# One fused kernel of six layers: first rows and job order of the scan, Silu, sums and store by halves, statistics behind the scan

## The chip, the cores and the metric

One Trainium2 chip, one NeuronCore. The metric is the device time of one execution in microseconds (us), as the median of several runs. Engines: PE multiplies matrices, DVE (VectorE) and POOL (GpSimd) do elementwise work, ACT (ScalarE) applies functions and copies, SP issues the DMAs. All run at once and wait for each other by semaphores.

## The reference

On x of 8 x 256 tokens with 256 features each, six layers in a row, each on a layernorm of x and added to it: a half-weighted mixture of experts, a Mamba layer with a selective scan, the same mixture again, a half-weighted SwiGLU feed-forward, causal attention with ALiBi, and the feed-forward again.

```python
x = x + 0.5 * moe(layernorm(x))
x = x + mamba(layernorm(x))
x = x + 0.5 * moe(layernorm(x))
x = x + 0.5 * ffn(layernorm(x))
x = x + attention(layernorm(x))
x = x + 0.5 * ffn(layernorm(x))

# moe, ffn: (silu(x @ Wg) * (x @ Wu)) @ Wd; the moe weights each expert's part by its gate
# the scan within mamba, for 512 channels and 16 states, over 256 steps of each sequence:
s = exp(delta * A) * s + delta * B * u
y = sum over states of s * C, then (y + D * u) * silu(gate) @ Wout
```

## The kernel before, in words

**Tiling.** The 2048 tokens are four chunks of 512; a chunk has two pairs of 128-token tiles. x stays in SBUF as tile X. The normed and transposed x is kept in two parts, high and low (xnT_hi, xnT_lo); a product is made of three matmuls, high by high, high by low, low by high (`three`, lines 161 to 163).

**Between two layers (class Tail).** A pair of tiles goes through `stats` on DVE (bn_stats, bn_aggr), `pool` (rstd by a power, on POOL), `norm` (DVE; in the scan's tail for chunks 0 and 1 it is ACT, lines 288 to 294, and POOL then has four operations in place of two), `pe` (transpose), `act` (the high part, a copy out of PSUM), `low` (DVE, the low part). The entry into the first layer is class Entry: `chunk` issues the loads of x by chunks on SP's queue, between the loads of the first weight tiles; `vector`, `scalar` and `tensor` are written out by hand in order, so their line order is each engine's order.

**Mixture and feed-forward (class Glu).** The hidden features come in tiles of 128: 25 tiles in 6 groups (2, 4, 4, 5, 5, 5) in a mixture, 8 in a feed-forward. A step j is one tile for one chunk: 100 steps in each mixture, 32 in each feed-forward. In a step, `gu` makes 12 matmuls of 512 columns: six into the gate half, then six into the up half; `down` makes 12 of 256 columns for the step before, into the sum banks 5 (first pair of tiles) and 6 (second pair). ACT takes Silu of the gate half (`scalar`, line 778). DVE multiplies with the up half; in tiles with gates (all but the first two of a mixture) it multiplies the up half with the gate rows first (line 827). ACT copies the high part (784), DVE makes the low part (850), and `down` of that step waits for it. `take` (DVE) adds the sum banks to X at the end of a chunk. After the last step of the kernel `Tail.sync` stores X chunk by chunk.

**The scan (class Scan).** 128 units q, 32 for each chunk c: 16 states for channels 0 to 255 (h = 0), then 16 for channels 256 to 511 (h = 1). r is q modulo 32. In a unit, ACT writes the decays into two PSUM banks (`decays`, two activations, line 1551), POOL writes the inputs into one of four state buffers (`inputs`, line 1208), DVE runs the recurrence (`scan`, line 1618) and multiplies with C (`weigh`, line 1625), for which PE has spread a row of C to all partitions (`spread`, line 1421), and PE sums the result over states (y, line 1437). PE's step q is: wait for weigh(q), spread(q + 1), y(q), then one *job* of the next or the last chunk, out of the tables `JOBS` (each pass), `START` (first chunk in its place) and `LAST` (last chunk). At n = 0 (r = 0 and 16) y also waits for the gate product (`gate`) that reads the sum of the half before.

**Jobs.** h, g: projections to the conv input and to the gate; v: the convolution, in two steps; xp, ms: projection and mean square for the norms; dt: step sizes; out: the output product of the chunk before (16 matmuls); ln: the tail's transpose. All use PSUM bank 7, one after the other: `vacant` waits until the job before has been read out of it (for g, by the Silu of `take` on ACT). v and g load the Silu table and load the other one again after it. A `DIAG` entry adds D * u to y after the job. ACT's order in a pass: decays(q + 2), take of the job of q - 1, then at fixed r `log` (three activations for the softplus), tail work. POOL's: `inputs(q + 3)`, with `lose`, `lost`, `step`, `times_u`, `normed`, `rows_lo` between, at fixed r. inputs(q) waits for y(q - 4), which frees its buffer.

**Where the scan hands over.** In the last chunk the tail's statistics of chunks 0 and 1 are made within the loop (r = 5, 12, 21, 23), as are POOL's rstd (r = 7, 14, 22, 24) and ACT's norm (r = 9, 16, 24, 26). After the loop PE makes the second mixture's first `gu`, then both output jobs, and DVE adds them. Chunks 1 to 3 are transposed in the mixture's first steps (class Reentry).

## Time and profile before

| | us |
|---|---|
| median of 3 runs | 1901.24 (1899.95 to 1901.25) |
| the profiled execution | 1902.52 |
| its span, by which the trace counts | 1900.7 |
| PE, DVE, ACT, POOL busy | 1808.4, 1333.8, 945.2, 581.2 |
| first mixture from, scan from, second mixture from | 12.8, 469, 970 |

Busy time is what an engine's instructions take; where it is full, nothing else can be sooner. A bracket behind a row of the timeline says how long the engine stood idle before it and what ended that. The mean granted clock of PE is 0.993 of full speed.

### The profile page before, as it was taken

To read this page: it belongs to the slowest core of one execution; us is meant where nothing else is said; L and a number is where in the kernel's file an instruction comes from. 1 tells how busy PE (TensorE), PEld (TensorE's weight loads), DVE (VectorE), ACT (ScalarE), POOL (GpSimd) and SP (SyncE) were. 2 spreads that over 40 slices of the span, in tenths; PEclk is the share of its full clock that TensorE was granted. 3 is DMA by queue.
4 is the path that set the end of the run, shared out by engine and by line. 5 is a ranking of instruction groups with operands and counts; after the bars stand their busy time and mean duration, and the time that the engine had idled before them with its cause. 6 is when DMAs were issued, how large, how long until landed. Compare 5 with 4: busy or idle time off the path is not lost.

```text
span 1900.7 us, 26241 instructions
## 1 busy us (share of the span) xinstructions
PE 1808.4 (95%) x9417; PEld 1375.2 (72%) x9417; DVE 1333.8 (70%) x1870; ACT 945.2 (50%) x1782; POOL 581.2 (31%) x399
## 2 busy tenths in 40 slices
PE   7999999999799999988689999999999999999998
PEld 6888888888354544534267888888888887777887
DVE  6666656567999999999976666565675556666533
ACT  3442323333688677684445433233333338888422
POOL 1000234000489878888720000000000025555000
PEclk9999999999899999999999999999999999999999
DMA  5332344220222222223202233232121306553100
GB/s 197 90 98 66 97 145 136 64 62 23 67 73 70 69 72 77 71 71 108 72 17 76 72 95 105 65 104 63 64 77 44 65 1 147 109 109 68 37 12 23
DMA packets 84186, 146.39 MB, mean 77 GB/s; under 512 B 13848, under 2 KB 23704, under 8 KB 83544
## 3 DMA queue, kind: packets, MB, share of 16 engines
q1 hardware_dynamic: 84056, 144.72, 26.6%
q8 instruction: 75, 1.23, 0.3%
q14 instruction: 55, 0.45, 0.1%
HBM read 130.38 MB, written 14.29 MB: 76 GB/s over the span
## 4 chain that ended last, share of the span: by engine, by line
PE 72%; DVE 14%; issue 6%; ACT 4%; POOL 3%; DMA 0%; DVEq 0%; SPq 0%; POOLq 0%; ACTq 0%
PE psum L161 19%; PE psum L162 18%; PE psum L163 18%; DVE scan_state L1618 6%; PE psum L1437 5%; POOL scan_state L1208 2%; PE psum L1990 1%; PE psum L1361 1%; DVE scan_state L1625 1%; PE psum L1332 1%; ACT attn_p L2138 1%; DVE X L807 1%; DVE moe_hidden_lo L850 1%; PE psum L1421 1%; PE psum L278 1%
## 5 line engine op out<-in xcount | busy, mean ns | idle before, releaser
L1208 POOL TENSOR_TENSOR scan_state<-scan_delta_u,scan_B_rows 128x1024 f32<-128x1024 f32 x127 | 299.5, 2368 | 95.3 <-PE psum L1437 81.2
L161 PE MATMUL psum<-xnT_hi,moe_w_hi 128*128 128x512 f32 x800 | 316.5, 396 | 2.7 <-DVE xnT_lo L470 2.6
L778 ACT ACTIVATE moe_hidden<-psum 128x512 f32<-128x512 f32 x200 | 119.5, 597 | 393.9 <-PE psum L163 393.9
L162 PE MATMUL psum<-xnT_lo,moe_w_hi 128*128 128x512 f32 x800 | 314.2, 393 | 0.0
L163 PE MATMUL psum<-xnT_hi,moe_w_lo 128*128 128x512 f32 x800 | 312.0, 390 | 0.0
L1618 DVE TENSOR_TENSOR_SCAN scan_state<-psum,scan_state 128x1024 f32<-128x1024 f32 x128 | 292.2, 2283 | 4.2 <-POOL scan_state L1208 3.0
L827 DVE TENSOR_TENSOR moe_gated_up<-moe_gate_rows,psum 128x512 f32<-128x512 f32 x184 | 126.5, 688 | 210.0 <-PE psum L163 124.8
L1437 PE MATMUL psum<-scan_state,ident 128*128 128x512 f32 x512 | 248.1, 608 | 3.8 <-DVE scan_gated L1633 2.6
L418 POOL TENSOR_SCALAR rstd<-mean_var 128x2 f32<-128x2 f32 x48 | 10.5, 220 | 752.8 <-DVE mean_var L452 752.5
L161 PE MATMUL psum<-moe_w_hi,moe_hidden_hi 128*128 128x256 f32 x800 | 230.4, 288 | 3.9 <-DVE moe_hidden_lo L850 2.6
L163 PE MATMUL psum<-moe_w_hi,moe_hidden_lo 128*128 128x256 f32 x800 | 226.3, 283 | 0.0
L162 PE MATMUL psum<-moe_w_lo,moe_hidden_hi 128*128 128x256 f32 x800 | 226.3, 283 | 0.0
L1551 ACT ACTIVATE psum<-scan_delta,scan_A 128x510 f32<-128x510 f32 x256 | 165.4, 679 | 117.5 <-DVE scan_state L1618 114.6
L784 ACT ACTIVATE moe_hidden_hi<-moe_hidden 128x512 fp32r<-128x512 f32 x200 | 126.3, 631 | 168.0 <-DVE moe_hidden L831 165.7
L850 DVE TENSOR_TENSOR moe_hidden_lo<-moe_hidden,moe_hidden_hi 128x512 fp32r<-128x512 f32 x200 | 138.2, 691 | 73.7 <-ACT moe_hidden_hi L784 72.1
L163 PEld LDWEIGHTS psum<-xnT_hi,moe_w_lo 128*128 128x128 f32 x800 | 150.7, 188 | 33.1
L161 PEld LDWEIGHTS psum<-xnT_hi,moe_w_hi 128*128 128x128 f32 x800 | 151.4, 189 | 30.1 <-issue 4.0
L162 PEld LDWEIGHTS psum<-xnT_lo,moe_w_hi 128*128 128x128 f32 x800 | 151.5, 189 | 24.1 <-issue 0.2
L161 PEld LDWEIGHTS psum<-moe_w_hi,moe_hidden_hi 128*128 128x128 f32 x800 | 152.5, 191 | 17.6 <-issue 6.3
L1625 DVE TENSOR_TENSOR scan_state<-scan_state,psum 128x1024 f32<-128x1024 f32 x128 | 156.2, 1220 | 7.0 <-PE psum L1421 3.0
L1437 PEld LDWEIGHTS psum<-scan_state,ident 128*128 128x128 f32 x512 | 98.3, 193 | 84.0 <-issue 69.5
L162 PEld LDWEIGHTS psum<-moe_w_lo,moe_hidden_hi 128*128 128x128 f32 x800 | 152.6, 191 | 7.8 <-issue 1.4
(226 smaller groups left out, 3476.4 us busy)
## 6 DMA issues: line engine op xcount, KB each, us to landing
scan_B_rows<-scan_B SPq DMA_DIRECT2D x127, 256.0 KB, 3.1
moe_gate_rows<-gate_table SPq DMA_DIRECT2D x176, 128.0 KB, 3.0
moe_w_raw<-moe_pack SPq DMA_DIRECT2D x50, 384.0 KB, 4.0
attn_stack<-attn_rows SPq DMA_DIRECT2D x96, 128.0 KB, 5.3
moe_gate_rows<-gate_table SPq DMA_DIRECT2D x32, 224.0 KB, 3.1
ffn_w_raw<-ffn_pack SPq DMA_DIRECT2D x16, 384.0 KB, 3.6
moe_gate_rows<-gate_table SPq DMA_DIRECT2D x32, 160.0 KB, 2.6
moe_gate_rows<-gate_table SPq DMA_DIRECT2D x24, 192.0 KB, 2.8
```

The lines of the kernel that those rows point to most:

```text
L161: e.matmul(out, wH, xH, start=start, stop=False)
L162: e.matmul(out, wH, xL, start=False, stop=False)
L163: return e.matmul(out, wL, xH, start=False, stop=stop)
L778: e.activation(self.hb[:, b, :], self.k.psum[:, 2 * b, :], ACT.Silu).then_inc(self.s_silu.sem, 1)
L784: e.activation(self.hH[:, b, :], self.hb[:, b, :], ACT.Copy).then_inc(self.s_hH.sem, 1)
L827: e.tensor_tensor(self.tu[:, b, :], self.gp[:, at, :], k.psum[:, 2 * b + 1, :], ALU.mult).then_inc(self.s_tu.sem, 1)
L850: e.tensor_tensor(self.hL[:, b, :], self.hb[:, b, :], self.hH[:, b, :].bitcast(F32), ALU.subtract).then_inc(self.s_hL.sem, 1)
L1208: e.tensor_tensor(self.st[q % self.NBUF][:], self.dtu[:, 2 * h:2 * h + 2, :], self.Bs[:, q % self.RING, :].unsqueeze(1).broadcast_to([P, 2 ...
L1437: x = e.matmul(ps[:, 4 + m, :], k.ident[:], self.st[q % self.NBUF][:, m, :], start=(n == 0), stop=(n == NST - 1))
L1551: x = e.activation(ps[:, 2 * (q % 2) + m, :].rearrange("p (s t) -> p s t", s=2)[:, :, 1:], self.delta[:, i, :].rearrange("p (s t) -> p s t ...
L1618: e.tensor_tensor_scan(st, ps[:, b:b + 2, :].rearrange("p b t -> p (b t)"), st, 0.0, ALU.mult, ALU.add).then_inc(self.s_scan.sem, 1)
L1625: e.tensor_tensor(st[:], st[:], ps[:, 6, :].unsqueeze(1).broadcast_to([P, 2, CHUNK]), ALU.mult).then_inc(self.s_z.sem, 1)
```

## The change

1. **Load.** x's first chunk comes as two loads of 256 rows with a semaphore each.
2. **Entry's order.** ACT splits the first weight tile before its first copy; DVE makes the low weight and both low parts before the statistics of chunk 1.
3. **Silu by half.** `gu` signals after the gate half (s_gs), and Silu waits for that; DVE waits for the whole (s_gu) in tiles without gates.
4. **Last sums and store by halves.** For the last chunk of the last layer the first pair of tiles is added once bank 5 is done, and each pair is stored by itself.
5. **Statistics behind the scan.** Those of chunk 1 come after the last gate, with POOL's rstd and ACT's norm in the next layer.
6. **Job order of the scan.** out1 from r = 10 to 6 (its sum from 12 to 8), v1 to 8 and 9, h2 and h3 to 10 and 11; g0, g1 of the first chunk from 10, 11 to 6, 7; g2, g3 from 25, 26 to 19, 25; h0, h1 from 29, 30 to 26, 29; the D products of channels 2, 3 from 19 to 20 and 21.
7. **n = 0.** At r = 0 and 16 the job comes before the wait for the gate and before y.

```diff
 # Tail
-        for c in range(NCH):
+        for c in range(NCH - 1):
             e.wait_ge(self.s_add.sem, self.s_add.at(2, c))
             e.dma_start(self.out[c * CHUNK:(c + 1) * CHUNK, :].rearrange("(n p) f -> p n f", p=P),
                         self.k.X[:, 4 * c:4 * c + 4, :]).then_inc(self.s_store.sem, 16)
-        e.wait_ge(self.s_store.sem, 16 * NCH)
+        for p in range(2):
+            e.wait_ge(self.s_add.sem, self.s_add.at(p + 1, NCH - 1))
+            rows = slice((TILES - 4 + 2 * p) * P, (TILES - 2 + 2 * p) * P)
+            e.dma_start(self.out[rows, :].rearrange("(n p) f -> p n f", p=P),
+                        self.k.X[:, TILES - 4 + 2 * p:TILES - 2 + 2 * p, :]).then_inc(self.s_store.sem, 16)
+        e.wait_ge(self.s_store.sem, 16 * (NCH + 1))
...
 # Glu
-        m.then_inc(self.s_gu.sem, 1)
+            m.then_inc((self.s_gu if half else self.s_gs).sem, 1)
...
+            if n == 1 and self.tail.last and j == self.N - 1:
+                m.then_inc(self.s_half.sem, 1)
...
-            e.wait_ge(self.s_gu.sem, self.s_gu.at(j + 1))
+            e.wait_ge(self.s_gs.sem, self.s_gs.at(j + 1))
...
+            if by_half and p == 0:
+                e.wait_ge(self.s_half.sem, self.s_half.at(1))
+            elif by_half:
+                e.wait_ge(self.s_dn.sem, self.s_dn.at(self.N))
...
             else:
+                e.wait_ge(self.s_gu.sem, self.s_gu.at(j + 1))
                 e.wait_ge(self.s_silu.sem, self.s_silu.at(j + 1))
...
 # Entry
+        if c == 0:
+            for p, sem in enumerate((self.tail.s_in[0], self.tail.s_in2)):
+                e.dma_start(self.k.X[:, 2 * p:2 * p + 2, :],
+                            self.x[p * 2 * P:(p + 1) * 2 * P, :].rearrange("(n p) f -> p n f", p=P)
+                            ).then_inc(sem.sem, 16)
+            return
...
+        self.moe.split_hi(e, 0)
         for p in range(2):
             self.tail.act(e, 0, 2 * p + 1)
-            self.moe.split_hi(e, p)
+        self.moe.split_hi(e, 1)
...
+        self.moe.split_lo(e, 0)
+        t.low(e, 0, 0)
+        t.low(e, 0, 1)
         t.add(e, 1, 0)
         t.stats(e, 1, 0)
-        t.low(e, 0, 0)
-        self.moe.split_lo(e, 0)
-        t.low(e, 0, 1)
...
 # Scan
-    JOBS = {0: ("dt2", 0), 1: ("dt3", 0), 2: ("out0", -1), 4: ("v0", 1, 0), 5: ("v0", 1, 1), 6: ("v1", 1, 0),
-            7: ("v1", 1, 1), 8: ("h2", 1), 9: ("h3", 1), 10: ("out1", -1), 12: ("v2", 1, 0), 13: ("v2", 1, 1),
+    JOBS = {0: ("dt2", 0), 1: ("dt3", 0), 2: ("out0", -1), 4: ("v0", 1, 0), 5: ("v0", 1, 1), 6: ("out1", -1),
+            8: ("v1", 1, 0), 9: ("v1", 1, 1), 10: ("h2", 1), 11: ("h3", 1), 12: ("v2", 1, 0), 13: ("v2", 1, 1),
             14: ("v3", 1, 0), 15: ("v3", 1, 1), 16: ("xp0", 1, 0), 17: ("xp0", 1, 1), 18: ("ms0", 1),
-            20: ("dt0", 1), 21: ("dt1", 1), 22: ("xp1", 1, 0), 23: ("xp1", 1, 1), 24: ("ms1", 1),
-            25: ("g2", 0), 26: ("g3", 0), 27: ("g0", 1), 29: ("h0", 2), 30: ("h1", 2), 31: ("g1", 1)}
-    START = {2: ("h0", 1), 3: ("h1", 1), 10: ("g0", 0), 11: ("g1", 0)}
-    DIAG = {0: (0,), 1: (1,), 19: (2, 3)}
+            19: ("g2", 0), 20: ("dt0", 1), 21: ("dt1", 1), 22: ("xp1", 1, 0), 23: ("xp1", 1, 1), 24: ("ms1", 1),
+            25: ("g3", 0), 26: ("h0", 2), 27: ("g0", 1), 29: ("h1", 2), 31: ("g1", 1)}
+    START = {2: ("h0", 1), 3: ("h1", 1), 6: ("g0", 0), 7: ("g1", 0)}
+    DIAG = {0: (0,), 1: (1,), 20: (2,), 21: (3,)}
...
             if n == 0 and q:
                 e.wait_ge(self.s_z.sem, self.s_z.at(q + 1))
                 spread(q + 1)
+                if self.job(q):
+                    job(self.job(q), self.BANK)
                 e.wait_ge(self.s_yg.sem, self.s_yg.at(2 * c + h))
...
-            if self.job(q):
+            if self.job(q) and (n or not q):
                 job(self.job(q), self.BANK)
...
-            if c and r in (4, 12):
+            if c and r in (4, 8):
                 add(c - 1, 0 if r == 4 else 1)
...
-            if c == NCH - 1 and r in (5, 12, 21, 23):
-                self.tail.stats(e, r // 20, int(r in (12, 23)))
+            if c == NCH - 1 and r in (5, 12):
+                self.tail.stats(e, 0, int(r == 12))
         gate(NCH - 1, 1)
+        for p in range(2):
+            self.tail.stats(e, 1, p)
         for p in range(2):
             add(NCH - 1, p, self.ENDS[p])
```

POOL's and ACT's tail work of chunk 1 leaves the scan's loop in the same way; `Glu.pool` of the second mixture starts at chunk 1, and `Reentry.act` makes ACT's norm of chunk 1 at its step 0, ahead of the copies.

## Rows read from the trace of the kernel before

**Rows 1.** The page: PE's busy tenths in 40 slices; one stretch of the busy times.

```profile
PE   7999999999799999988689999999999999999998
...
469.00:970.00 501.00, 446.34 (x1175) 212.61 (x1173) 478.14 (x325) 347.58 (x475) 385.34 (x186) 0.97 0.23 71
```

**Rows 2.** Chain of waits (first row) and timeline, 0 to 13: start, length, engine, line.

```profile
1.43 3.81 DMA X<-x
...
8.65 2.04 PE L278 MATMUL psum<-ident,x_stage 128*128 128x128 f32 x8 [8.65 <-DVE x_stage L460]
...
10.27 0.83 ACT L751 ACTIVATE moe_w_hi<-moe_w_raw 128x768 fp32r<-128x768 f32 x1
...
11.00 0.59 ACT L298 ACTIVATE xnT_hi<-psum 128x512 fp32r<-128x512 f32 x1
...
12.84 0.77 PE L161 MATMUL psum<-xnT_hi,moe_w_hi 128*128 128x512 f32 x1 [2.15 <-DVE xnT_lo L470]
```

**Rows 3.** Timeline of DVE in the scan: two recurrences, one unit apart.

```profile
558.10 2.28 DVE L1618 TENSOR_TENSOR_SCAN scan_state<-psum,scan_state 128x1024 f32<-128x1024 f32 x1
...
561.55 2.28 DVE L1618 TENSOR_TENSOR_SCAN scan_state<-psum,scan_state 128x1024 f32<-128x1024 f32 x1
```

**Rows 4.** Timeline of DVE in the scan: its longer waits.

```profile
611.44 2.29 DVE L1618 TENSOR_TENSOR_SCAN scan_state<-psum,scan_state 128x1024 f32<-128x1024 f32 x1 [0.97 <-POOL scan_state L1208]
...
630.66 0.69 DVE L1638 TENSOR_TENSOR X<-X,psum 128x512 f32<-128x512 f32 x1 [1.68 <-PE psum L1361]
...
660.17 0.69 DVE L1638 TENSOR_TENSOR X<-X,psum 128x512 f32<-128x512 f32 x1 [1.31 <-PE psum L1361]
...
747.77 0.69 DVE L1638 TENSOR_TENSOR X<-X,psum 128x512 f32<-128x512 f32 x1 [0.31 <-PE psum L1361]
```

**Rows 5.** Chunk boundary: PE's busy time and granted clock; y; ACT's Silu of g1.

```profile
616.00:620.00 4.00, 3.83 (x5) 0.59 0.26 95
734.00:738.00 4.00, 3.36 (x8) 1.00 0.30 106
...
616.17 3.24 PE L1437 MATMUL psum<-scan_state,ident 128*128 128x512 f32 x4 [0.64 <-DVE scan_gated L1633]
...
616.37 0.60 ACT L1494 ACTIVATE scan_silu_gate<-psum 128x512 f32<-128x512 f32 x1
```

**Rows 6.** First chunk: y in the chain of waits; ACT's decays, and a g.

```profile
523.35 1.72 PE psum L1437 x4
...
525.32 1.30 ACT L1551 ACTIVATE psum<-scan_delta,scan_A 128x510 f32<-128x510 f32 x2
...
545.02 0.60 ACT L1494 ACTIVATE scan_silu_gate<-psum 128x512 f32<-128x512 f32 x1
545.63 1.28 ACT L1495 ACT_TABLE_LOAD   x1
```

**Rows 7.** Timeline of POOL: the inputs that start its chain of 11 operations.

```profile
585.30 2.36 POOL L1208 TENSOR_TENSOR scan_state<-scan_delta_u,scan_B_rows 128x1024 f32<-128x1024 f32 x1 [1.59 <-PE psum L1437]
```

**Rows 8.** Timeline of DVE: statistics within the loop; the last output's sum.

```profile
931.75 0.75 DVE L448 BATCH_NORM_STATS2 bn<-X 128x6 f32<-128x256 f32 x2
...
932.75 2.29 DVE L1618 TENSOR_TENSOR_SCAN scan_state<-psum,scan_state 128x1024 f32<-128x1024 f32 x1
...
976.67 0.69 DVE L1638 TENSOR_TENSOR X<-X,psum 128x512 f32<-128x512 f32 x1 [4.98 <-PE psum L1361]
```

**Rows 9.** The end: chain of waits (first row), timeline; stores by size and us to landing.

```profile
1890.26 0.23 PE psum L161
...
1894.41 0.39 PE L161 MATMUL psum<-ffn_w_hi,ffn_hidden_hi 128*128 128x256 f32 x1 [1.37 <-DVE ffn_hidden_lo L850]
...
1896.15 1.29 DVE L807 SCALAR_TENSOR_TENSOR X<-psum,X 128x512 f32<-128x512 f32 x2 [1.79 <-PE psum L163]
...
out<-X SPq DMA_DIRECT2D x4, 512.0 KB, 2.8
attn_rows<-attn_rows_hi SPq DMA_DIRECT2D x16, 256.0 KB, 2.0
```

More of the change, by code:

```diff
@@ L197, in __init__ @@
         if entry:
+            self.s_in2 = Sem(k, "in0b")
             self.s_in = [Sem(k, f"in{c}") for c in range(NCH)]
@@ L433, in add @@
             e.wait_ge(self.s_in[c].sem, self.s_in[c].at(16))
+            if c == 0 and p:
+                e.wait_ge(self.s_in2.sem, self.s_in2.at(16))
         if not self.back:
@@ L533, in __init__ @@
         self.s_gu = Sem(k, "gu", total=N)
+        self.s_gs = Sem(k, "gs", total=N)
         self.s_silu = Sem(k, "silu", total=N)
@@ L539, in __init__ @@
         self.s_dn = Sem(k, "dn", total=N)
+        self.s_half = Sem(k, "dn_half") if tail.last else None
         self.s_acc = Sem(k, "acc", total=NCH * (self.NG - 1))
@@ L656, in pool @@
     def pool(self, e):
-        for c in range(2 if self.guest else NCH - 1 if self.handed else NCH, NCH):
+        for c in range(1 if self.guest else NCH - 1 if self.handed else NCH, NCH):
             for slot in (0, 2):
@@ L801, in take @@
         c, last = n % NCH, n - NCH * (self.NG - 1)
-        e.wait_ge(self.s_dn.sem, self.s_dn.at(self.ends(n)))
+        by_half = self.tail.last and n == NCH * self.NG - 1
+        if not by_half:
+            e.wait_ge(self.s_dn.sem, self.s_dn.at(self.ends(n)))
         if n >= NCH:
@@ L1004, in pe, with act @@
         super().pe(e, j)
+    def act(self, e, j):
+        if j == 0:
+            for p in range(2):
+                self.tail.act(e, 1, 2 * p)
+        super().act(e, j)
 class Scan:
@@ L1233, in pool @@
                 self.next.split_lo(e, q + 5 - self.N)
-            if c == NCH - 1 and r in (7, 14, 22, 24):
-                self.tail.pool(e, r // 20, 2 * (r in (14, 24)))
+            if c == NCH - 1 and r in (7, 14):
+                self.tail.pool(e, 0, 2 * (r == 14))
         if not self.next:
@@ L1589, in scalar @@
                 log(c + 1, 0)
-            if c == NCH - 1 and r in (9, 16, 24, 26):
-                self.tail.act(e, r // 20, 2 * (r in (16, 26)))
+            if c == NCH - 1 and r in (9, 16):
+                self.tail.act(e, 0, 2 * (r == 16))
             if r == 27 and c + 1 < NCH:
@@ L1679, in vector @@
                 gate((q - 1) // self.UNITS, 0 if r else 1)
-            if c == NCH - 1 and r in (5, 12, 21, 23):
-                self.tail.stats(e, r // 20, int(r in (12, 23)))
+            if c == NCH - 1 and r in (5, 12):
+                self.tail.stats(e, 0, int(r == 12))
         gate(NCH - 1, 1)
+        for p in range(2):
+            self.tail.stats(e, 1, p)
         for p in range(2):
```

## The prediction

> **What bounds the kernel now.** I read the busy times first. In the mixtures of experts and the feed-forwards (slices 2 to 9, 21 to 32 and 38 to 39 of 40) PE's digit is 9, so an edit pays there only where PE stands: at the start, at a seam, at the end. In the scan DVE is full (478 of 501 us) and PE is not (446) [rows 1]. Then I read each stage's timeline. To PE's first projection, at 12.84, a chain runs from the load of x over statistics, transposes and ScalarE's copies [rows 2]. In the scan one unit of DVE (recurrence, weighting) starts every 3.45 us [rows 3], and only a few rows show DVE standing [rows 4]. In the last 9 us one tile's chain drains alone [rows 9]. The sum is made against the profiled execution (1902.5 us, span 1900.7), which lies 1.3 above the median of 1901.24; I apply it to the median. A measurement of this kernel tells about 0.2%, 3.8 us, from no change.
>
> **First rows.** The load of 512 KB takes 3.81 us [rows 2]. Halved, its first half can land sooner by up to its share of the moving time; I take 0.7 (bounds 0 and 1.3), the second no sooner, and SP issues one DMA more (0.4 us), behind which the first weight tile still lands before ACT wants it. Statistics and rstd of pair 0 move forward, pair 1 follows on POOL, so both transposes come 0.7 sooner. ACT now splits the weight ahead of its copies: before, the split (0.83 from 10.27) held the second copy back to 11.00, though its transposes ended at 10.69 [rows 2]. DVE had statistics and the low weight ahead of the second low part and now has only the weight, done while the copy runs. So that low part (0.7), which PE waits for, ends at 10.75 + 0.6 + 0.7 = 12.05, with the load's share at 11.4, and no longer at 12.8: PE starts 1.3 sooner. That stretch runs at the lower clock, and the clock need not rise sooner with it, and DVE owes two pairs of statistics (1.0 each, by [rows 8]), one norm and one split before the first product, which it then reaches some 1.2 sooner. **-1.2** (-0.6 to -1.6); PE carries it through the first mixture.
>
> **Silu by half.** 232 steps get an earlier Silu, but PE is full there [rows 1], and gated tiles wait for DVE's own product anyway: nothing, while PE's queue covers it. It counts where PE has run dry: at the second mixture's start, -0.3 (0 to -0.7), and at the end. There PE stood 1.37 for the chain Silu, product, high, low [rows 9]. Silu (0.6) leaves that chain: -0.65. The last sums: two instructions in 1.29 after PE's last matmul; half of it now runs beside PE's second half: -0.6. Store: 512 KB lands in 2.8, a store of 256 KB in 2.0 [rows 9]; half remains at the end: -0.5 (0 to -0.8). **-1.75**.
> The Trainium skill (DMA: Bandwidth & Descriptors, Anatomy of one DMA) puts most of a DMA's fixed cost in its completion, which halving does not shorten; by that rule only the moving time of half the bytes goes.
>
> **Statistics behind the scan.** Two pairs leave DVE's loop in the last chunk, 1.00 each from 931.75 to 932.75. They go between the last gate and the last sums, where DVE stands 4.98 [rows 8]. POOL's and ACT's share go with them, into 6 us in which both stand. **-2.0**, and covered: 2.0 fits in 5. Without that cover they would cost the same again.
>
> **Job order of the scan.** Four things, by step r of 32.
> (a) r = 0: the job moves ahead of y and of the wait for the gate. Before, PE stood there 0.6, and DVE later waited 1.68 for the output job [rows 4]. But the job dt2 takes the bank of g1, the job of r = 31, whose Silu runs at 616.37 to 616.97 [rows 5]. So PE cannot do the job in the gap: it stands until 617.0, then job and y. Against the old course (y from 616.17) that is worth 1.0 if PE is at its full clock, as y took 3.24 in place of 1.72 at a granted clock of 0.59. At the second boundary the clock stayed at 1.00 [rows 5], the later wait was 0.31 [rows 4], and there it costs 0.7. So: -1.35 over three boundaries with the clock up in all, +3.65 with it down in all (1.7 each). PE stands longer than before, which speaks for down; I take **+1.1**.
> The Trainium skill (TensorE: Matmul & The Clock Gate, Part 1) says that the clock follows recent activity and that its phase varies from run to run. By that rule each boundary is a throw; the rows agree in that two alike idles gave different clocks.
> (b) out1 from r = 10 to 6, its sum from 12 to 8. DVE waited 1.31 for it in two chunks [rows 4], PE being late after six full steps; now two are ahead. Bounds 0 and 1.31 each; I leave 0.9: **-0.9** in all.
> (c) Chunk 0: g0, g1 move to r = 6, 7, behind log (r = 5) and v0. A g costs ACT its Silu and two table loads, 3.2, and the decays 1.3, over the unit's 3.45 [rows 6]. ACT: decays at 525.32, + 1.3 + load 1.3 + Silu 0.6: g0 leaves its bank at 528.5; second load, decays, load, Silu: g1 at 533.0. PE: y ends at 525.07, + projection 1.4 (six matmuls of 0.23 [rows 9]) + spread 0.2 + y 1.7: it wants g0's bank at 528.4, and by the same steps g1's at 532.0. PE is full in this chunk, so this 1.1 goes to DVE: **+1.1** (0 to 2.2).
> The Trainium skill (ScalarE: Activation LUTs, What ACT_TABLE_LOAD costs) counts 2.66 us for each switch with its drain. The rows show the next ACTIVATE 1.3 after a load starts; by the page (c) would be some 5 us.
> (d) g2 moves to 19, the two D products to 20 and 21, and at r = 16 the job stands ahead of y but waits 0.9 for v3's Silu. PE then is 0.5 to 0.8 later at y of step 23. That y starts POOL's chain: it waited 1.59 for it at 585.30 [rows 7], is then busy through 11 operations, and DVE waits 0.97 for its last [rows 4]. What y loses, DVE loses: **+1.8** over three chunks (0 to 2.5). That g2 is out of ACT's crowd at 26 to 28 helps only a wait that this one covers.
>
> **Sum:** -1.2 - 0.3 - 1.75 - 2.0 + 1.1 - 0.9 + 1.1 + 1.8 = -2.15; 1901.24 becomes **1899.1**. The bounds of this course reach from about -6 to +2.
>
> **Rival A, the scan's new order pays.** The clock holds at all boundaries (-1.35), chunk 0 absorbs ACT's crowd, POOL's chain starts where it did, and (b) gives all but 1.1: then the scan gives -1.35 - 1.5, the statistics -2.0, and start, seam and end -3.25 to -4.3: some -8.5, about 1893; with half of it, 1895. For it: the PE's slack of a unit (a spread is due only 2.3 us after its release, as long as a recurrence takes [rows 3]). Against it: the Silu rows of [rows 5, 6]. 28%.
>
> **Rival B, slower: PE's new waits take the clock.** Place: r = 0 and r = 16, where a job held for an eviction now stands ahead of y. At r = 0 PE stands 1.6 on end, at r = 16 0.9. If both bring the low clock, a boundary costs as in (a), +3.65, and at r = 16 PE falls 1.7 further behind, to 3 us against the 2.3 that a spread has: DVE loses 0.8 each in four chunks, 3.2, and POOL's chain starts later, +1.5. With (c), (d) and (b): +3.65 + 1.1 + 1.8 - 0.9 + 3.2 + 1.5 = 10.35, less 5.25 elsewhere: +5.1, 1906.3. It decides where the low clock comes at more than the three boundaries. For it: two of three are low already. Against: at the second boundary PE stood 0.6 of 4 us and kept its full clock [rows 5]. 7%.
>
> **Rival C, the start and the end do not pay.** The clock rises at the same time as before whatever starts sooner, x's halves land together, and the last store completes with its latency: the start gives 0.3, the end 1.0. Then -0.5: 1900.7. 12%, all of it within 0.2%.
>
> **Numbers.** The forecast has 53%, with C and A's weak part within 3.8 us: faster by over 0.2% 30% (A and the forecast's lower tail), within 62%, slower 8%. The range leaves out the far ends of A and B: 1894.3 to 1903.8.
>
> **What would show it.** PE's first projection near 11.5 and the Silu of it before its second half ends; dt2's bank wait at each boundary ending on scan_silu_gate, and the clock there; waits for L1361 at the second sum below 1.3; PE waits on scan_silu_gate in 528 to 533; DVE's wait for POOL before step 32 above 0.97; no stall at the seam beyond 5 us for the moved statistics; the last store alone behind 1896. I am wrong if DVE's waits in the scan shrink in sum by over 4 us, or if PE waits nowhere for an eviction.

## The result, and the profile after

The changed kernel takes 1906.55 us (1905.25 to 1907.61) where the kernel before, on the same chip, took 1901.96 (1899.95 to 1905.45): a ratio of 1.0021, 95% interval 1.0011 to 1.0030. Measured again on another chip it was 1906.03 against 1903.32, 1.0018 (1.0009 to 1.0027). It is slower, by 2.7 to 4.6 us (0.2%), where 1899.1 and 2.15 us faster were forecast, and it lies outside the range of 1894.3 to 1903.8. The profiled execution took 1905.30, its span 1903.2, 2.5 more than the span of before.

**The start and the end** did what they should. First the timeline of the changed kernel's start (start, length, engine, line, operation, in brackets the idle time before it and what ended it):

```profile
4.33 0.75 DVE L456 BATCH_NORM_STATS2 bn<-X 128x6 f32<-128x256 f32 x2 [4.33 <-DMA X<-x]
...
7.61 2.04 PE L279 MATMUL psum<-ident,x_stage 128*128 128x128 f32 x8 [7.61 <-DVE x_stage L468]
...
8.73 0.60 ACT L299 ACTIVATE xnT_hi<-psum 128x512 fp32r<-128x512 f32 x1
...
9.69 0.60 ACT L299 ACTIVATE xnT_hi<-psum 128x512 fp32r<-128x512 f32 x1 [0.36 <-PE psum L279]
...
11.11 0.77 PE L161 MATMUL psum<-xnT_hi,moe_w_hi 128*128 128x512 f32 x1 [1.46 <-DVE xnT_lo L478]
```

PE transposes at 7.61 where [rows 2] had 8.65, the second copy starts at 9.69 where it was 11.00, and the first projection comes 1.73 sooner. Then the last waits, timeline of PE and DVE, and of the page's DMA issues the last store's (x count, size of one, us to landing):

```profile
1898.25 0.39 PE L161 MATMUL psum<-ffn_w_hi,ffn_hidden_hi 128*128 128x256 f32 x1 [0.74 <-DVE ffn_hidden_lo L869]
...
1899.27 1.41 DVE L825 SCALAR_TENSOR_TENSOR X<-psum,X 128x512 f32<-128x512 f32 x2 [1.07 <-PE psum L163]
```

```profile
out<-X SPq DMA_DIRECT2D x2, 256.0 KB, 2.1
```

PE stands 0.74 for its last hidden tile where [rows 9] had 1.37, the sums start while PE still works (DVE waited 1.07, not 1.79), and half a store lands in 2.1, not 2.8.

**The scan** took it all back. One stretch of it, PE's busy time (and number of instructions), then PEld, DVE, ACT, POOL, then granted clock, DMA share and GB/s:

```profile
468.00:974.00 506.00, 443.10 (x1170) 212.37 (x1168) 475.43 (x316) 344.28 (x469) 382.34 (x178) 0.98 0.22 70
```

The stretch is 5 us longer than that of [rows 1], and DVE is busy 475 us of it, no more than before: it waits more. DVE's longer waits now, in its timeline:

```profile
533.70 1.22 DVE L1659 TENSOR_TENSOR scan_state<-scan_state,psum 128x1024 f32<-128x1024 f32 x1 [1.42 <-PE psum L1453]
...
623.47 1.22 DVE L1659 TENSOR_TENSOR scan_state<-scan_state,psum 128x1024 f32<-128x1024 f32 x1 [0.99 <-PE psum L1453]
...
632.23 0.69 DVE L1672 TENSOR_TENSOR X<-X,psum 128x512 f32<-128x512 f32 x1 [1.68 <-PE psum L1393]
...
647.75 0.69 DVE L1672 TENSOR_TENSOR X<-X,psum 128x512 f32<-128x512 f32 x1 [1.14 <-PE psum L1393]
```

The first is in chunk 0, behind g0 and g1; the others follow the first chunk boundary: the weighting of step 2 (0.99, new), the sums of out0 (1.68, as in [rows 4]) and out1 (1.14; 1.31 before). The views that put numbers on all of it are the starts of the 128 recurrences: a step takes 3.45 us [rows 3], so what lies between two starts beyond that is what DVE lost or did besides. "The gap at step r" is the time from the start of recurrence r to that of r + 1, less 3.45. Summed by place, in us, from the timelines of three kernels (the third is the run undo_order, below):

```
                                        before   changed   undo_order
start of the first recurrence           495.44    493.41     494.36
chunk 0, steps 0 to 15                    2.15      3.89       1.42
steps 25 to 31, chunks 0 to 2             4.61      7.05       4.61
steps 2 to 4 of chunks 1, 2, 3       2.57 0.88 2.56  3.42 3.42 3.15  0.88 0.88 0.88
second output's sum, chunks 1 to 3        4.43      4.07       4.43
statistics in chunk 3                     4.0       2.0        2.0
first to last recurrence                469.42    475.25     463.28
last low part to the end of the span      7.01      5.70       5.72
```

The scan's gaps account for 5.8 of the 5.83 us that it is longer. The statistics' 2.0 are gone from it as planned, so the new order costs 7.8 (0.28 of it is the gap at step 2 of chunk 0, which differs from run to run, see the last section). The biggest row is that of the three boundaries, 9.99 where it was 6.01. One of them, PE and ACT from the changed kernel's timeline:

```profile
615.74 0.50 PE L1453 MATMUL psum<-scan_BC,scan_state_pick 128*128 128x512 f32 x1 [1.38 <-DVE scan_state L1659]
617.73 1.15 PE L1385 MATMUL psum<-scan_weighted,scan_Wdt 128*128 128x512 f32 x2 [1.49 <-ACT scan_silu_gate L1528]
618.70 3.58 PE L1471 MATMUL psum<-scan_state,ident 128*128 128x512 f32 x4
```

```profile
615.79 1.28 ACT L1528 ACT_TABLE_LOAD   x1
617.08 0.60 ACT L1528 ACTIVATE scan_silu_gate<-psum 128x512 f32<-128x512 f32 x1
```

and PE's busy time and granted clock in three stretches around it:

```profile
611.00:615.00 4.00, 3.37 (x11) 1.00 0.19 66
615.00:619.00 4.00, 1.76 (x4) 0.96 0.45 121
619.00:623.00 4.00, 4.00 (x7) 0.61 0.30 76
```

PE stands 1.38 for the weighting, then 1.49 for g1's Silu, which frees dt2's bank, and right behind that the clock falls to its lower level (1.2 GHz) and y takes 3.58. PE stands 1.49 for the Silu at the other two boundaries too. There the clock falls while dt2 runs: its two matmuls take 1.92 and 2.08, not 1.15, and y 2.82 and 2.40. The second profile of the changed kernel shows the same three. Before, y took 3.24 at the first [rows 5] and 3.61 at the third, and 1.99 at the second.

### The profile page after: what moved, and what is told of

Same layout as the page of the kernel before. It is cut to its first block, busy times and chain, and to the rows that moved or that the text cites. A ratio compares the mean times of both kernels' runs of the same rounds, so it can differ in the third digit from the quotient of the medians.

```text
span 1903.2 us, 26321 instructions
## 1 busy us (share of the span) xinstructions
PE 1807.4 (95%) x9417; PEld 1376.8 (72%) x9417; DVE 1333.9 (70%) x1870; ACT 945.9 (50%) x1782; POOL 579.5 (30%) x399
## 4 chain that ended last, share of the span: by engine, by line
PE 73%; DVE 13%; ACT 6%; issue 5%; POOL 2%; DMA 1%; SPq 0%; DVEq 0%; ACTq 0%; POOLq 0%
PE psum L161 19%; PE psum L162 19%; PE psum L163 18%; DVE scan_state L1652 5%; PE psum L1471 5%; PE psum L1393 1%; PE psum L2026 1%; PE psum L1373 1%; POOL scan_state L1240 1%; ACT attn_p L2174 1%; DVE moe_hidden_lo L869 1%; PE psum L1385 1%; DVE X L825 1%; DVE scan_state L1659 1%; PE psum L279 1%
```

## The experiments

Base is the changed kernel, where no other is named. The time of the kernel before behind each "against" was taken on the same chip; where a text says how far a run lies from the changed kernel, that is a difference of medians of different chips, on which the kernel before read 1901.96 to 1904.20. A "low boundary" is one at which the clock is at its lower level while y or the job ahead of it runs: y takes 2.4 to 3.6 us in place of 1.9 to 2.0, and the gap at step 4 is 2.25, in place of 0.88 (or 1.7, where the job is held).

**undo_order**: the whole of the scan's order back.

```diff
-    JOBS, START, DIAG as changed;  if c and r in (4, 8): add(...)
-                if self.job(q):                      # ahead of y at n == 0
-                    job(self.job(q), self.BANK)
+    JOBS, START, DIAG as before;   if c and r in (4, 12): add(...)
+            if self.job(q):                          # behind y
```

Expected:

> The changed kernel with the scan's order as before (job table, first chunk's table, D products, the second output sum at step 12, the job of steps 0 and 16 behind y); start, seam, end, Silu by half and the statistics behind the scan stay changed. Theory (the scan's order is what costs): the gaps between recurrences go back to those of before but for the two statistics, so the scan gives back 7.8 us of the changed kernel's span: 1897.5 to 1899.5, 3 us below the kernel before, with fewer than three boundaries at the low clock. Rival (the earlier start moves the phase of the clock's windows, and that alone brings the low clock to all three boundaries): all three boundaries still low, gaps of the second boundary still 3 us, time about 1903.

Measured: 1893.91 us against 1903.53 of the kernel before, 0.9957 (0.9944 to 0.9969); span 1891.7. The gaps are the table's third column, no boundary is low. The scan is 12.0 shorter than the changed kernel's (463.28 against 475.25), more than the 7.8 expected, since the kernel before had two low boundaries in its profile and this one none (3.4), and the gap at step 2 of chunk 0 was 0.40, for 1.13 (0.7). The rival (the earlier start takes the clock) falls: the start is the same, the clock is up. PE at that boundary, and the three stretches again:

```profile
613.29 0.50 PE L1453 MATMUL psum<-scan_BC,scan_state_pick 128*128 128x512 f32 x1 [0.97 <-DVE scan_state L1657]
614.42 1.98 PE L1469 MATMUL psum<-scan_state,ident 128*128 128x512 f32 x4 [0.63 <-DVE scan_gated L1665]
```

```profile
611.00:615.00 4.00, 2.40 (x9) 1.00 0.43 111
615.00:619.00 4.00, 4.00 (x11) 1.00 0.45 117
619.00:623.00 4.00, 4.00 (x11) 1.00 0.24 80
```

**only_order**: the kernel before with the new order alone.

> The kernel before with the scan's new order alone (tables, D products, sum at step 8, job ahead of y). Theory (the order costs whatever stands around it): three boundaries at the low clock, the scan about 7.8 us longer than before, 1909 to 1910.5. Rival (the phase that the earlier start brings takes the clock): one or two boundaries low, 1905 or less.

Measured: 1913.38 against 1903.53, 1.0062 (1.0049 to 1.0074). Three boundaries low, each with gaps of 0.96 (0.74 at the third), 0.21 and 2.25; from the first to the last recurrence 477.19, 7.77 more than before. So the order costs this whatever stands around it, and the profile's 7.8 are it. The median is 9.9 above before, and beyond the 1909 to 1910.5 expected; the span is 10.1 above, and the 2.3 outside the scan lie in the attention (1.75), the start (0.36) and the second mixture (0.25), which this edit does not touch.

**undo_job0**: only the job of steps 0 and 16 goes back behind y.

```diff
                 spread(q + 1)
-                if self.job(q):
-                    job(self.job(q), self.BANK)
                 e.wait_ge(self.s_yg.sem, self.s_yg.at(2 * c + h))
...
-            if self.job(q) and (n or not q):
+            if self.job(q):
```

> The changed kernel, only the job of steps 0 and 16 goes back behind y. Theory (the job held for the gate's Silu is what delays y and takes the clock): the waits of 0.99 at the weighting of step 2 go, and at one or more of the three boundaries the clock stays up: 3 to 4.5 us less than the changed kernel, 1902 to 1903.5. Rival (the tables, not the job's place, cost the time; the boundaries are low at random): at most 1 us less, 1905.5 or more.

Measured: 1900.29 (1896.88 to 1902.51) against 1903.53, 0.9987 (0.9978 to 0.9995). 5.7 to 6.3 us less than the changed kernel, more than I expected. One boundary of three is low (gaps 0.11, 0.21, 2.25), two have 0.88; the new gap of 0.96 is gone everywhere. Besides, the gap at step 25 falls from 0.49 and 0.25 to 0.06: that part belongs to the job of step 16.

**job_alone**: the opposite, the old tables and only the job ahead of y (the base is undo_order).

> The run undo_order's kernel (old tables), and of the scan's changes only the job of steps 0 and 16 ahead of y. Theory (dt2, held for g1's Silu, keeps PE standing 1.5 us ahead of y; that costs 0.85 at the weighting of step 2 and takes the clock each time): three of three boundaries at the low clock with a gap of 0.96 at step 2 and 2.25 at step 4, 7.5 us more than undo_order: 1901 to 1902. Rival (the empty step 30 of the new table, where PE stands 1.25 more, takes the clock, not the held job): boundaries low in at most one of three, 2.5 to 4 us more, 1897 to 1898.

Measured: 1900.49 against 1904.20, 0.9982 (0.9973 to 0.9991); span 1898.3, 6.6 above undo_order. Second and third boundary low with 0.96, 0.21, 2.25 as expected; the first kept its clock and lost 0.84 all the same:

```profile
612.80 0.50 PE L1453 MATMUL psum<-scan_BC,scan_state_pick 128*128 128x512 f32 x1 [0.97 <-DVE scan_state L1659]
614.78 1.12 PE L1385 MATMUL psum<-scan_weighted,scan_Wdt 128*128 128x512 f32 x2 [1.48 <-ACT scan_silu_gate L1528]
615.75 1.88 PE L1471 MATMUL psum<-scan_state,ident 128*128 128x512 f32 x4
```

So the price of the held job is now known from both sides: the gap at step 4 is 1.72 for 0.88 with the clock up (+0.84), and the gaps are 3.42 in all for 0.88 with it low (+2.54). The tables' empty step 30 is not needed for it.

**g1_earlier**: the changed kernel, two table entries swapped, so that a plain copy and not a Silu is the last to leave dt2's bank.

```diff
-            ... 27: ("g0", 1), 29: ("h1", 2), 31: ("g1", 1)}
+            ... 27: ("g0", 1), 29: ("g1", 1), 31: ("h1", 2)}
```

> The changed kernel with g1 at step 29 and h1 at step 31, so that dt2's bank is freed by a copy of 0.6 and no longer by a Silu behind a table load of 1.3. Theory: PE's stand of 1.49 ahead of dt2 goes to 0.3 or less, the gap of 0.96 at step 2 goes at all boundaries, and some of them keep the full clock: 2.5 to 6 us less than the changed kernel, 1900.5 to 1904. Rival (PE stands at the boundary anyway, for DVE's weighting and the gate): low at all three, gaps as they were, 1906.

Measured: 1898.21 (1897.02 to 1898.87) against 1904.20, 0.9974 (0.9963 to 0.9985), 8 us below the changed kernel, more than expected. No boundary is low: the gaps there are 2.63 in all, for 9.99, and that is 7.4 of the 8.35 by which the scan is shorter; the other 1.0 is the gap at step 2 of chunk 0, not of this edit. PE and ACT at the first:

```profile
615.71 0.50 PE L1453 MATMUL psum<-scan_BC,scan_state_pick 128*128 128x512 f32 x1 [1.36 <-DVE scan_state L1659]
616.30 1.13 PE L1385 MATMUL psum<-scan_weighted,scan_Wdt 128*128 128x512 f32 x2
617.27 1.88 PE L1471 MATMUL psum<-scan_state,ident 128*128 128x512 f32 x4
```

```profile
615.68 0.58 ACT L1512 ACTIVATE scan_conv_in<-psum 128x512 f32<-128x512 f32 x1
```

The weighting's 1.36 is unchanged, the 1.49 is gone, y starts 1.4 sooner and runs in 1.88. This is the run that shows the hold to be the cause: these two entries are all that differs. At the third boundary step 31 has no job (h1 has no chunk left), so PE stood 2.77 in one piece for the weighting, then not again, and the clock stayed up there too.

**undo_start, undo_tail, undo_out1**: one part of the tables back each, in the changed kernel.

```diff
 undo_start
-    START = {2: ("h0", 1), 3: ("h1", 1), 6: ("g0", 0), 7: ("g1", 0)}
+    START = {2: ("h0", 1), 3: ("h1", 1), 6: ("v1", 1, 0), 7: ("v1", 1, 1), 8: ("h2", 1), 9: ("h3", 1),
+             10: ("g0", 0), 11: ("g1", 0)}
 undo_tail
-            19: ("g2", 0), ... 25: ("g3", 0), 26: ("h0", 2), 27: ("g0", 1), 29: ("h1", 2), 31: ("g1", 1)}
+            25: ("g2", 0), 26: ("g3", 0), 27: ("g0", 1), 29: ("h0", 2), 30: ("h1", 2), 31: ("g1", 1)}
-    DIAG = {0: (0,), 1: (1,), 20: (2,), 21: (3,)}
+    DIAG = {0: (0,), 1: (1,), 19: (2, 3)}
 undo_out1
-            6: ("out1", -1), 8: ("v1", 1, 0), 9: ("v1", 1, 1), 10: ("h2", 1), 11: ("h3", 1)
+            6: ("v1", 1, 0), 7: ("v1", 1, 1), 8: ("h2", 1), 9: ("h3", 1), 10: ("out1", -1)
-            if c and r in (4, 8):
+            if c and r in (4, 12):
```

> The changed kernel, only the first chunk's table goes back (g0, g1 at steps 10 and 11 behind v1, h2, h3). Theory: the gap of 1.38 at step 10 of chunk 0 and 0.2 behind it go, the first 16 steps take 1.6 to 1.8 us less: 1904.5 to 1905.2. Rival (ACT's crowd only moves, since g0 and g1 cost ACT the same wherever they stand): 0.3 or less, no difference in the first 16 steps.

Measured: 1904.83 against 1903.53, 1.0011 (1.0002 to 1.0020). The first 16 steps take 57.52, for 59.09: 1.57 less, the gap of 1.39 at step 10 gone (0.12 of it is the gap at step 2 and not of this edit, so the two g cost 1.45). Just below the 1.6 to 1.8 expected. In the changed kernel ACT's timeline there reads

```profile
524.91 1.28 ACT L1528 ACT_TABLE_LOAD   x1
526.20 0.60 ACT L1528 ACTIVATE scan_silu_gate<-psum 128x512 f32<-128x512 f32 x1
526.82 1.28 ACT L1529 ACT_TABLE_LOAD   x1
528.12 1.30 ACT L1585 ACTIVATE psum<-scan_delta,scan_A 128x510 f32<-128x510 f32 x2
529.43 1.28 ACT L1528 ACT_TABLE_LOAD   x1
530.73 0.60 ACT L1528 ACTIVATE scan_silu_gate<-psum 128x512 f32<-128x512 f32 x1
```

and PE waits for g1's Silu:

```profile
531.38 1.99 PE L1364 MATMUL psum<-scan_conv_in,scan_taps 128*128 128x512 f32 x4 [0.90 <-ACT scan_silu_gate L1528]
```

> The changed kernel with the tables of steps 16 to 31 and the D products as before (g2, g3 at 25 and 26, h0, h1 at 29 and 30, both products at 19). Theory: POOL's chain starts earlier again and the gap at step 31 falls from 1.5 to 1.1 and the one of 0.25 to 0.5 at step 25 to under 0.1; step 30 has its job back; the held job still takes the clock at all three boundaries: 2.0 to 2.7 us less than the changed kernel, 1904. Rival (without the empty step 30 PE stands less and the clock holds): one boundary or none low, 1900 or less.

Measured: 1903.50 against 1904.20, 1.0001 (0.9992 to 1.0010); about 2.5 to 3 below the changed kernel. The gaps of steps 25 to 31 are 4.59 over three chunks for 7.05: 2.5. Two of three boundaries low (the first kept its clock, gap 1.71, y 1.88 behind a stand of 1.49). So the full step 30 does not save the clock, and the rival falls as it was stated. A share of it is not excluded: with the new tables' empty step 30, PE standing 1.34 to 1.39 for the weighting, 15 of 15 held boundaries in this study are low; with step 30 full (undo_tail, job_alone), where that stand is 0.87 to 0.97, 4 of 6. The last chunk has a low stretch besides, behind one stand of PE of 2.25 at step 6 (granted clock 0.64 in 878 to 881), with a gap of 2.36 at step 8.

> The changed kernel with out1 back at step 10 and its sum at step 12, v1, h2, h3 two steps up as before (the first chunk's table unchanged). Theory (the sum's wait is the length of the output job itself, wherever it stands): a gap of 1.9 at step 12 in place of 1.7 at step 8, no more: 0.4 us over three boundaries, the same time as the changed kernel, 1906.5 to 1907. Rival (my forecast, two steps ahead give DVE 0.3 to 0.5 each time against the 1.31 of before): 1.2 us or more later.

Measured: 1906.04 against 1904.20, 1.0015 (1.0006 to 1.0023), the changed kernel's time. The gap at step 12 is 1.88 for 1.70 at step 8, DVE's wait 1.31 for 1.14. That is all that the two steps ahead give: 0.18 in each of two chunks, and in the third nothing, since the sum there loses 0.67 wherever it stands.

**entry_back, silu_back, end_back, stats_back**: undo_order's kernel with one of the four other parts undone, each by the diff of the change.

> The kernel with the scan's old order and the other parts changed (the run undo_order), in which only the first rows go back too: x's first chunk in one load, ACT's and DVE's order at the start as before. Theory (first rows give 1 to 2 us by themselves and do not touch the clock of the scan): the first recurrence at 495.4, 1.1 to 2.0 us later than with them, time 1895 to 1896, and of the three boundaries of the scan as few at the low clock as in undo_order. Rival (the earlier start sets the clock's phase, and with it the boundaries): boundaries low again, 1898 or more.

Measured: 1896.05 (1895.29 to 1899.02) against 1903.30, 0.9962 (0.9947 to 0.9976). PE transposes at 8.63 and projects at 12.86, as before; first recurrence at 496.15, for 494.36; no boundary low. Theory holds: the start does not set the scan's clock.

> The run undo_order's kernel, in which only the Silu by half is undone (ACT waits for both halves of the projection). Theory: PE's waits for the hidden low part grow by 0.6 at each of the places where its queue has run dry, the end among them: 0.65 at the end and 0.3 to 0.6 at a seam, 1895.0. Rival (232 steps gain and PE idles less overall): 3 us or more later, 1897.

Measured: 1897.75 (1895.27 to 1900.42) against 1903.30, 0.9967 (0.9956 to 0.9979). In the trace, PE's last wait is back:

```profile
1891.03 0.39 PE L161 MATMUL psum<-ffn_w_hi,ffn_hidden_hi 128*128 128x256 f32 x1 [1.37 <-DVE ffn_hidden_lo L867]
```

the last feed-forward takes 0.62 more. The first feed-forward loses more than the theory had: its last two waits are back too. Here the first of them, in silu_back and then in undo_order:

```profile
1541.55 0.39 PE L161 MATMUL psum<-ffn_w_hi,ffn_hidden_hi 128*128 128x256 f32 x1 [1.71 <-DVE ffn_hidden_lo L867]
...
1537.54 0.39 PE L161 MATMUL psum<-ffn_w_hi,ffn_hidden_hi 128*128 128x256 f32 x1 [1.09 <-DVE ffn_hidden_lo L869]
```

The second is 1.37 for 0.74, and with 0.35 ahead of them this feed-forward ends 1.6 later. With 0.15 at the second mixture's start Silu by half is worth 2.4 us in the rows. The median lies 3.0 to 3.8 above undo_order's, as the rival had it, but the profile also has two low boundaries, and the runs spread over 5 us. How much of the 1.6 comes through the attention behind it no single profile tells, as the next section says.

> The run undo_order's kernel, in which only the last sums and the last store are undone (one wait for both sums, one store of 512 KB). Theory: from the last low part to the end 7.0 less the Silu's 0 to 0.6, in place of 5.7: 1.1 us later, 1895.0. Rival (a store completes with its fixed latency): 0.5 or less.

Measured: 1896.50 (1894.91 to 1901.06) against 1903.30, 0.9966 (0.9953 to 0.9978). From the last low part to the end it takes 7.00, for 5.72: 1.28. The rival (0.5 or less) falls.

> The run undo_order's kernel, in which only the second two pairs of statistics go back into the scan's last chunk. Theory: two gaps of 1.0 come back at steps 21 and 23, the seam behind loses its 0.7 of delay at the next mixture's gathered rows: 1.3 us net, 1895.2. Rival (they would fit into the scan's idle time or the wait at its end takes the whole back): 2.0 or 0.

Measured: 1896.57 against 1903.30, 0.9964 (0.9949 to 0.9978). The gaps of 1.00 at steps 21 and 23 are back. From the last recurrence to the low part of the next mixture's step 4 it takes 39.28, for 39.24 with the statistics behind: they were covered in full there. The expected 0.7 at the mixture's gathered rows did not come back either (79.35 and 79.16 over the next 16 steps), so that delay is not theirs.

**swap_old, swap_only**: undo_order's kernel (old tables) with g1 at step 30 and h1 at 31, the job ahead of y or behind it.

```diff
-            ... 29: ("h0", 2), 30: ("h1", 2), 31: ("g1", 1)}
+            ... 29: ("h0", 2), 30: ("g1", 1), 31: ("h1", 2)}
```

> The run undo_order's kernel with g1 at step 30, h1 at step 31, and the job of steps 0 and 16 ahead of y: the bank is free when dt2 comes. Theory (the stand's length decides the clock; PE's order around y is worth nothing by itself): no boundary low, gaps 0 at step 2 and 0.88 at step 4 as in undo_order, 1893 to 1894.5 and narrower than undo_order. Rival (the job ahead fills the gate's gap and y is no later, so DVE's wait for the output job shrinks): the gap at step 4 below 0.6, 1 us or more less than undo_order.

> The run undo_order's kernel with g1 at step 30 and h1 at step 31 only, the job of steps 0 and 16 behind y. Theory: the same gaps as undo_order, since no one waits for dt2's bank with the job behind y; 1893.5 to 1895, with a low boundary now and then, as PE still stands 0.95 and 0.64 there. Rival (ACT's Silu two table loads earlier delay other evictions): a new gap of 0.3 or more at steps 30 or 31 in each chunk, 1 us more.

Measured: swap_old 1893.51 (1892.85 to 1896.23), swap_only 1894.42 (1893.90 to 1896.67) against 1904.12: 0.9951 (0.9939 to 0.9964) and 0.9954 (0.9940 to 0.9968). swap_old has no low boundary, and its gap at step 4 is 0.88: the job ahead of y gains nothing even where its bank is free, it only moves PE's work from behind y to before it. Its runs are no narrower than undo_order's, against my expectation. swap_only has two low boundaries of three, with the old 0.11, 0.21, 2.25. Both beat either kernel; swap_old has the lowest median of this study, level with undo_order within the intervals.

**undo_order_again, before_again, after_again**: second profiles.

> The same kernel as undo_order, a second profile and three more rounds. Theory (its freedom from low boundaries was partly chance; PE stands there as long as in the kernel before): some runs 1.5 to 4 us above 1893.9, median 1893.5 to 1896. Rival (something in the changed parts keeps the clock up): all runs within 1893 to 1895.5 again.

> The kernel before, a second profile. Theory (the low clock at a boundary is chance where PE stands 0.95 and 0.64): another number of low boundaries than two, or others of the three, with gaps of 0.88 where the clock is up and 2.57 in all where it is low. Rival: the first and third low again, the second up.

> The changed kernel again. Theory (the parts add up; a held job brings the low clock at 16 of 18 boundaries): two or three boundaries low in the profile, with gaps of 0.96, 0.21 and 2.25 behind each, and a median 2 to 4 us above the kernel before on the same chip. Rival (the difference of 4.6 of the first measurement holds, and the parts do not add up): 4.5 us or more above before.

Measured: undo_order_again 1894.74 (1893.44 to 1896.55) against 1904.12, one boundary low (the first), none in the first profile. before_again 1906.74 in one run, one boundary low (the first; two before). after_again 1906.03 against 1903.32, three low again, with the first profile's gaps to 0.02.

The boundaries of all 19 profiles of the study together:

| PE's order at the boundary | PE stands, us | low boundaries | cost of one, up / low |
|---|---|---|---|
| job behind y (before and nine others) | 0.8 to 1.4 (once 2.3), then 0.64 | 9 of 30 | 0.88 / 2.57 |
| job ahead of y, held for the Silu (changed and six others) | 0.9 to 1.4, then 1.49 | 19 of 21 | 1.7 / 3.1 to 4.7, mostly 3.42 |
| job ahead of y, bank free (g1_earlier, swap_old) | 0.9 to 1.4 (third boundaries 2.3 and 2.8), then 0 to 0.1 | 0 of 6 | 0.88 / none |

The dear ones, 4.5 (undo_start, first boundary) and 4.7 (undo_out1, third), are those at which both dt2 (2.08) and y (3.62) ran wholly at the lower level.

## Why the prediction was wrong

The mechanisms were named, nearly all came, and the sum failed on one term above all. Against the profile of before, by the prediction's own terms:

| term | forecast | measured | how |
|---|---|---|---|
| first rows | -1.2 | -2.0 | first recurrence 495.44 to 493.41 |
| Silu at the second mixture's start | -0.3 | -0.2 | last recurrence to step 4's low part, 39.43 to 39.26 |
| Silu in the first feed-forward | no term | -1.6 | silu_back |
| end (Silu; sums and store) | -0.65, -1.1 | -0.62, -1.3 | silu_back, end_back |
| statistics behind the scan | -2.0 | -2.0 | gaps, stats_back |
| (a) job ahead of y | +1.1 | +4.0 | 9.99 less 6.01 |
| (b) out1 at step 6 | -0.9 | -0.36 | undo_out1 |
| (c) g0, g1 in chunk 0 | +1.1 | +1.45 | undo_start |
| (d) g2, D products, step 16 | +1.8 | +2.4 | undo_tail |
| sum | -2.15 | -0.2 | span: +2.5 |

The remaining 2.8 of the profile lie where the change touches nothing: 0.28 in the gap at step 2 of chunk 0, 0.75 in steps 5 to 20 of the second mixture, 1.7 in the attention. These stretches differ as much between the two profiles of the kernel before (1.13 and 1.62; 78.49 and 79.49; 194.5 and 198.0, from the last sum of the first feed-forward to the last one's first product), and the profile that the forecast was read from has the lower value in each. The other one's span, 1904.9, even lies above the changed kernel's 1903.2: it is the medians, not the two profiles, that show the sign. Nor does one profile show whether the first feed-forward's 1.6 comes through the attention. From the first product of that feed-forward to that of the last one it takes 340.41 on average in the four profiles with the old Silu (339.04 to 342.47), and 339.15 in the fifteen with the new: 1.3 less.

**Term (a) is the step that failed**, and in it the choice, not the mechanism. I had written that the job is held for g1's Silu until 617.0, that PE stands longer, and that this speaks for the low clock, with a bound of +3.65 if it came at all three boundaries (by its own terms, 3 times 1.7 over -1.35, it is 3.75); then I took +1.1, near the middle, by treating the clock as an even throw. It was not: with the held job 19 of 21 boundaries are low, with the job behind y 9 of 30. The sizes within the term were right: the hold costs 0.84 with the clock up (forecast 0.7) and 1.70 more with it low (forecast 1.7). The measured +4.0 (0.85, 2.54 and 0.59 at the three) is a little beyond my bound. And the kernel before was priced by one profile with two low boundaries, an unlucky one by 9 of 30: against a mean boundary of before, (a) costs 3 times 0.84 and 3 times 1.69 times (0.90 less 0.30), 5.6 us. With it the terms make +1.3. The medians' 2.7 and 4.6 lie above that, by 1.4 and 3.3 us that no run here ties to a term.

(b) was missed for one reason: I let PE's lateness cause the wait. The sum waits 1.14 to 1.31 wherever both stand, two steps apart, so lateness is not the cause; that it is the length of the output job itself fits this and was not tested. (c) and (d) (the latter at 2.4 of 2.5) came within their bounds. In (c) the chain of [rows 6] held to 0.3 us: g1's bank came free at 531.3, forecast 533.0 less the 2.0 that all is earlier, and PE waited 0.90 for it, forecast 1.0; DVE then stood 1.42, which is the gap of 1.39 at step 10. In (d) the two causes were told apart: the job of step 16 waits only 0.55 to 0.6 for v3's Silu, not 0.9, the gap at step 25 is its part (0.06 without it), and the rest is g2, the D products and the order of h0 and h1, which no run tells apart; POOL's last operation ahead of step 32 is waited for 1.4, for 0.97.

**Silu by half** was priced at nothing wherever PE is full, and at the first feed-forward's last tiles it is not: PE stood 1.71 and 1.37 there for the low part, and stands 1.09 and 0.74 now. **The first rows** gave 0.8 more: the load's first half let DVE start 1.0 sooner, not 0.7. Over the fifteen profiles with the new start the first recurrence is at 493.9 on average (493.15 to 495.08), over the four without at 495.9 (495.44 to 496.39). One reading of [rows 1] was off, and nothing hung on it: slice 21 reads 8, not 9.

**The rules weighed.** On the store the rule of the Trainium skill (DMA: Bandwidth & Descriptors, Anatomy of one DMA) that the fixed cost stays, which that section states for a DMA issued from GpSimd, agrees with the trace of these stores from SP: half the bytes took 0.7 off the 2.8, and 2.1 remained. On (c), the rule of the Trainium skill (ScalarE: Activation LUTs, What ACT_TABLE_LOAD costs) of 2.66 us a switch would, by the prediction's estimate, have made some 5 us; the rows show the next ACTIVATE 1.29 after the load starts (524.91 to 526.20), and 1.45 was lost: here the measurement decides. On (a), the rule of the Trainium skill (TensorE: Matmul & The Clock Gate, Part 1) that the clock follows recent activity held, and its other half, that the phase varies from run to run, was the one I leaned on: 9 of 30 bear it out, 19 of 21 do not.

**The rivals.** Rival B gave 1906.3, and 1906 is what came, at a chance of 7%. That the number fits is luck: 4.7 us of its sum did not happen. Half of its mechanism is shown: the held job takes the clock at step 0. Its other half is not: the clock stayed up at step 16 and no low stretch came beyond the boundaries' three in the changed kernel's scan, but for the scan's first rows, where every profile has one; the gap at step 16 is 1.14 as before. In its place came (b), (c) and (d) at 1.5 more than forecast, and what differs from run to run. A fell with the boundaries, C with the start and the end, which paid more than they were forecast to. Of the signs that I had named, PE's wait for scan_silu_gate at each boundary, the waits in 528 to 533, the 0.97 grown to 1.4, the last store and the covered statistics (DVE stood 2.95 behind them) all showed; the sum's sign did not.

Left open: undo_order's runs lie 9.4 to 9.6 below before. Its four parts in the rows give 7.7 (2.0, 2.4, 1.3, 2.0), if the first feed-forward's 1.6 comes through in full, and the low boundaries' luck, at 9 in 30 for both kernels, at most 1.5. Part by part the medians give 1.3 to 3.8 each, with low stretches elsewhere in the scan's last chunk and the attention that no run here tied to a part.

## What to carry to other kernels

Where PE waits, price the wait twice: its length, and the chance that it brings the low clock, and that chance is not even. Where a stand of this length is added right ahead of a long run of matmuls, to one that already gives the low level at times, price the low level as sure. One profile is one draw of it: take two before a forecast of 2 us is built on one. When work is moved ahead of a wait to fill a gap, look first at who frees the buffer that it needs, and in what order that engine works: here two table entries swapped were worth 8 us, of which 1 is not theirs.

## What the runs showed of the hardware that was not expected

The clock's answer to PE's stand is steep. With 0.8 to 1.4 and 0.64 of standing around one short matmul three boundaries in ten came at the low level; with 1.49 in place of 0.64, nine in ten; with 0.1 or less, none of six (at three in ten, that would have a chance of 12%). The sum of the stands does not decide alone: at the third boundaries of g1_earlier and swap_old PE stood 2.77 and 2.31 in one piece and kept its full clock, where 1.34 to 1.39 and then 1.49 (2.8 to 2.9 in sum) gave the low level 15 times of 15. That is two cases, and undo_tail has one low stretch behind a single stand of 2.25, so the rule behind it stays open. Short stands by themselves cost nothing: in the changed kernel's last chunk PE works 4.43 of 8 us (892 to 900), standing 1.24 in every step, at a granted clock of 1.00.

The gap at step 2 of the first chunk goes from 0.08 to 1.66 between profiles of the same instructions there. It follows the moment at which the clock rises behind PE's stand at the scan's start. In all 19 profiles the first 6 us from the start of the first recurrence are at 0.50, the lower level. In the next 2 us the seven profiles with a gap of 0.08 to 0.42 were granted 0.86 falling to 0.68, in the order of their gaps. The other twelve, with gaps of 1.04 to 1.66, still had 0.50. This alone is worth up to 1.6 us between two runs and explains part of the spread of 5 us that the kernel before shows.
